# Expert stage of a mixture-of-experts block: four gather buffers instead of two, slots of four experts found ahead, late gathers in halves

## What is computed

```python
logits = x_flat @ Wr                                  # 12544 x 8
probs = softmax(logits, axis=0)                       # over the tokens
vals, idx = top_k(probs.T, 1024)                      # each of 8 experts picks 1024 tokens
selected = x_flat[idx]                                # gather
h = gelu(einsum('ecd,edf->ecf', selected, W1) + b1)   # 128 -> 512
out_e = einsum('ecf,efd->ecd', h, W2) + b2            # 512 -> 128
output = zeros.at[idx].add(vals[..., None] * out_e)   # scatter with add
```

## Time and profile before

| what | value |
|---|---|
| median of 3 runs | 534.93 us (534.64 to 538.28) |
| the profiled execution's own time | 540.0 us |
| its span, first to last instruction | 538.1 us |
| PE busy | 373.2 us (69%) |
| DVE busy | 320.3 us (60%) |
| ACT busy | 271.8 us (51%) |
| POOL busy | 167.6 us (31%), nearly all of it after 279 us |

### The profile page before, as it was taken

One profiled execution on the slowest core, in us unless ns is written; L12 is line 12 of the kernel. 1 busy time (PEld: TensorE's weight loads), 2 busy tenths in 40 slices (PEclk: granted clock), 3 DMA queues, 4 the chain that ended last, 5 costly groups with the idle time before them and its releaser, 6 DMA issues. The chain is left out here.

```text
span 538.1 us, 6516 instructions
## 1 busy us (share of the span) xinstructions
PE 373.2 (69%) x1532; PEld 227.4 (42%) x1532; DVE 320.3 (60%) x1059; ACT 271.8 (51%) x581; POOL 167.6 (31%) x153
## 2 busy tenths in 40 slices
PE   2989998999989976300026497897969595950565
PEld 2655665666666555200023253354434242410454
DVE  4578999999999885688864255444444220220354
ACT  3357888989889956766501246244435433400000
POOL 3000000000000000000017258787878788768000
PEclk9989999999999986555556699978879697995555
DMA  3413665454565333500002023434525243333898
GB/s 97 124 56 121 204 194 177 151 179 155 173 192 180 122 122 114 152 1 0 0 5 57 21 76 36 91 35 90 74 51 78 45 81 43 31 31 34 222 383 354
DMA packets 33957, 58.56 MB, mean 109 GB/s; under 512 B 5864, under 2 KB 18320, under 8 KB 33936
## 3 DMA queue, kind: packets, MB, share of 16 engines
q1 hardware_dynamic: 20016, 43.15, 25.4%
q0 software_dynamic: 11264, 8.66, 12.2%
q10 hardware_dynamic: 2656, 6.51, 3.2%
HBM read 28.02 MB, written 23.86 MB: 96 GB/s over the span
## 5 line engine op out<-in xcount | busy, mean ns | idle before, releaser
L374 POOL DMA_INDIRECT picked<-token_rows,gather_idx x64 | 62.0, 968 | 305.8 <-issue 292.1
L388 POOL DMA_INDIRECT moe_sum<-y_rows,scatter_idx x64 | 100.4, 1569 | 23.9 <-issue 23.3
L619 PE MATMUL psC<-x_pad,tap_diag 128*128 128x392 f32 x256 | 93.4, 509 | 8.9 <-ACT x_pad L515 8.8
L787 PE MATMUL psC<-hid,w 128*128 128x512 f32 x128 | 66.2, 676 | 0.4 <-issue 0.3
L900 DVE SCALAR_TENSOR_TENSOR conv<-x_pad,taps_w,conv 128x784 f32<-128x784 f32 x64 | 66.0, 1032 | 0.2
L619 PEld LDWEIGHTS psC<-x_pad,tap_diag 128*128 128x128 f32 x256 | 47.2, 194 | 40.6 <-ACT x_pad L515 7.9
L1181 DVE TENSOR_SCALAR y_T<-psC,b_T 128x256 f32<-128x256 f32 x32 | 14.0, 480 | 68.0 <-PE psC L787 68.0
L568 ACT ACTIVATE hid<-psB,b_T 128x512 f32<-128x512 f32 x32 | 22.0, 687 | 58.0 <-PE psB L778 38.1
L787 PEld LDWEIGHTS psC<-hid,w 128*128 128x128 f32 x128 | 27.6, 223 | 34.0 <-issue 34.0
L778 PE MATMUL psB<-picked_T,w 128*128 128x512 f32 x64 | 35.6, 668 | 9.2 <-ACT picked_T L548 8.9
L484 ACT ACTIVATE ln_tok<-psA,ln_sm 112x128 f32<-112x128 f32 x112 | 40.5, 459 | 2.7 <-DVE ln_sm L892 2.7
(11 more groups left out here) (195 smaller groups left out, 657.6 us busy)
## 6 DMA issues: line engine op xcount, KB each, us to landing
token_rows<-rows SPq DMA_DIRECT2D x16, 416.5 KB, 3.0
x_in<-in_x_dram SPq DMA_DIRECT2D x16, 392.0 KB, 3.7
x_res<-in_x_dram SPq DMA_DIRECT2D x16, 392.0 KB, 4.6
moe_sum<-zero_rows SPq DMA_DIRECT2D x16, 392.0 KB, 5.1
x_all<-x SPq DMA_DIRECT2D x16, 392.0 KB, 2.9
out_dram<-act ACTq DMA_DIRECT2D x16, 392.0 KB, 5.7
w<-in_L_ffn_W_dram SPq DMA_DIRECT2D x16, 256.0 KB
ln_tok<-moe_sum SPq DMA_DIRECT2D x8, 392.0 KB, 5.6
```

What stands on the lines that cost most here:

```text
L374: nc.gpsimd.indirect_dma_start(out=picked[:, q, b, :], out_offset=None, in_=rows_dram, in_offset=bass.IndirectOffsetOnAxis(ap=gather_idx[: ...
L388: nc.gpsimd.indirect_dma_start(out=y_dram, out_offset=bass.IndirectOffsetOnAxis(ap=scatter_idx[:, q, b:b + 1], axis=0), in_=y_rows[:, q, b ...
L619: ins = nc.tensor.matmul(psC[:, h, 0:HALF].rearrange("c (h w) -> c h w", w=W), tap_diag[:, n, :], x_pad_v[:, q, y0:y0 + LINES, dx:dx + W], ...
L787: ins = nc.tensor.matmul(psC[:, h, :], w2[:, q, f * C:(f + 1) * C], hid[:, f, h * HS:(h + 1) * HS], start=(f == 0), stop=(f == FT - 1))
```

## The change

- There are four gather buffers: the two of `picked`, and two made of `x_in` and `x_res`, which are free by then. Buffer is e % 4, and each has its own two semaphores.
- Indices have a place of their own for each expert (`slot_idx`), so the copy to `scatter_idx` and its waits go.
- Slots of experts 0 to 3 are found ahead on DVE. On PE, `ties(2)` and the first `turn_picked` come after all of expert 1's slots; the rest of the small matmuls of experts 2 and 3 stands in the two halves of expert 0's `hidden`. Experts 1 to 4 then find the slots of experts 4 to 7.
- POOL's order: gathers 0 to 3; scatter 0; gather 4; scatter 1; gather 5; scatter 2; first half of gather 6; scatter 3; second half of 6; scatter 4; first half of 7; scatter 5; second half of 7; scatter 6; scatter 7.
- Scatter 0 is a plain indirect write, without the add (`moe_sum` is zero then).
- In expert 6, `turn_picked` of expert 7 stands after `down` and `back`, and `down` and `back` go by halves; DVE's `weigh` follows that order.
- Python loops take the place of the chip's loops in the expert stage, on every engine.

```diff
+        slot_idx = sb("slot_idx", [128, E, SB], U32)
+        picked_in = [picked[:, 0, :, :], picked[:, 1, :, :]] + [
+            spare[:, :, :].rearrange("s q n -> s (q n)")[:, 0:SB * ROW].rearrange("s (b r) -> s b r", r=ROW)
+            for spare in (x_in, x_res)]
...
+            def gather(e, h):
+                k = e % AHEAD
+                if e >= AHEAD and h == 0:
+                    pool.wait_ge(s_pt, (e - AHEAD) * 2 + 2)
+                    pool.wait_ge(s_ge, e - AHEAD + 1)
+                pool.wait_ge(s_idx, e * 2 + h + 1)
...
+                    if e == 0:
+                        nc.gpsimd.indirect_dma_start(out=y_dram, out_offset=at, in_=y_rows[:, q, b, :],
+                                                     in_offset=None).then_inc(s_sca[q], 16)
+                    else:
+                        nc.gpsimd.indirect_dma_start(out=y_dram, out_offset=at, in_=y_rows[:, q, b, :],
+                                                     in_offset=None, compute_op=ALU.add).then_inc(s_sca[q], 16)
...
+            for e in range(AHEAD):
+                gather(e, 0)
+                gather(e, 1)
+            for e in range(3):
+                scatter(e)
+                gather(e + AHEAD, 0)
+                if e < 2:
+                    gather(e + AHEAD, 1)
+            scatter(3)
+            gather(6, 1)
+            scatter(4)
+            gather(7, 0)
+            scatter(5)
+            gather(7, 1)
+            scatter(6)
+            scatter(7)
...
-                if e:
-                    turn_picked(0, 0, 0, 0)
                 slot_ranks(e)
+            pe.wait_ge(s_idx, 4)
+            ties(2)
+            turn_picked(0, 0)
...
+                    slot_work, slots_of = {}, e + 3
+                    if e == 0:
+                        if h == 1:
+                            turn_picked(0, 1)
+                        slots_of = 2 + h
+                        slot_work = ({0: [slots_before], 3: [slot_ranks]},
+                                     {0: [first_ties], 1: [slots_before], 3: [slot_ranks]})[h]
+                    elif e + 3 < E:
+                        slot_work = ({2: [first_ties]}, {0: [slots_before], 3: [slot_ranks]})[h]
+                    hidden(e, q, h, slot_work, slots_of)
...
+                if e == E - 2:
+                    for h in range(2):
+                        turn_picked(e + 1, h)
...
-                nc.vector.tensor_copy(scatter_idx[:, q, :], gather_idx[:, q, :]).then_inc(s_si, 1)
```

More of the change, by code:

```diff
@@ L47 @@
 UNROLL = 5
+AHEAD = 4
 ENDS = 4
@@ L311, in _ @@
                 load_w(q, q)
[L312 to L315, removed]
+            for e in range(2, E):
+                sp.wait_ge(s_l2, (e - 1) * 2)
+                load_w(e, e % 2)
             sp.wait_ge(s_sca[0], 16 * SB * E // 2)
@@ L367, in _, with scatter @@
                            allow_small_or_imprecise_dtypes=True).then_inc(s_const, 1)
[L369 to L373, removed]
-                    nc.gpsimd.indirect_dma_start(
[L375 to L383, removed]
+            def gather(e, h):
[4 more added lines that the diff above has]
+                pool.wait_ge(s_idx, e * 2 + h + 1)
+                pool.sem_inc(s_pool, 1)
+                for b in range(4 * h, 4 * h + 4):
+                    nc.gpsimd.indirect_dma_start(
+                        out=picked_in[k][:, b, :], out_offset=None, in_=rows_dram,
+                        in_offset=bass.IndirectOffsetOnAxis(ap=slot_idx[:, e, b:b + 1], axis=0),
+                    ).then_inc(s_gat[h][k], 16)
+            def scatter(e):
+                q = e % 2
+                if e >= 1:
+                    pool.wait_ge(s_sca[1 - q], (e + 1) // 2 * (16 * SB))
                 for b in range(SB):
@@ L585, in _ @@
             act.wait_ge(s_sd, 9)
-            for q in range(2):
-                expert(q, q, 0, True)
-            with act.Fori(1, E // 2 - 1) as pair:
-                for q in range(2):
-                    expert(pair * 2 + q, q, pair, True)
-            for q in range(2):
-                expert(E - 2 + q, q, E // 2 - 1, q == 0)
+            for e in range(E):
+                expert(e, e + 1 < E)
             with act.Fori(0, B // ENDS) as turn:
@@ L780, in hidden @@
                     if f in after:
-                        after[f](e + 2)
+                        for work in after[f]:
+                            work(slots_of)
             def down(e, q, h):
@@ L823, in expert @@
                         down(e, q, h)
-                        back(e, h, another)
-            for q in range(2):
-                expert(q, q, 0, True, True)
-            with pe.Fori(1, E // 2 - 1) as pair:
-                for q in range(2):
-                    expert(pair * 2 + q, q, pair, True, True)
-            for q in range(2):
-                expert(E - 2 + q, q, E // 2 - 1, False, q == 0)
+                        back(e, h, False)
+                if e == E - 2:
+                    for h in range(2):
+                        turn_picked(e + 1, h)
+            for e in range(E):
+                expert(e, e % 2)
             pe.wait_ge(s_gelu, E * 2 * FT)
@@ L1165, in slots_d @@
                     dve.wait_ge(s_pd, e * 4 + 2 * h + 2)
[L1166 removed]
+                    nc.vector.scalar_tensor_tensor(slot_idx[:, e, blocks], s_p[:, blocks], float(TILES), ranks[:, blocks, P],
                                                    ALU.mult, ALU.add).then_inc(s_idx, 1)
[L1169 removed]
+            for e in range(AHEAD):
                 slots_a(e)
@@ L1207, in expert @@
                 bias_out(e, 0)
-                if last:
+                if e >= E - 2:
                     weigh(e, q, use, 0)
                 bias_out(e, 1)
-                if not last:
+                if e < E - 2:
                     weigh(e, q, use, 0)
                 weigh(e, q, use, 1)
-            for q in range(2):
-                expert(q, q, 0, True)
-            with dve.Fori(1, E // 2 - 1) as pair:
-                for q in range(2):
-                    expert(pair * 2 + q, q, pair, True)
-            for q in range(2):
-                expert(E - 2 + q, q, E // 2 - 1, False, q == 1)
+            for e in range(E):
+                expert(e, e % 2, e // 2)
             for q in range(2):
```

99 lines of the change are left out of this document (34 added, 65 removed).

## The result

| | before | after |
|---|---|---|
| median of 20 runs, us | 536.62 (534.19 to 538.54) | 532.90 (529.89 to 538.14) |
| ratio after / before, 95% interval | | 0.9929 (0.9911 to 0.9947) |
| profiled execution, us (span) | 540.0 (538.1) | 534.26 (532.5) |
| end of the last scatter, us | 498.10 | 491.87 |

The kernel is 3.7 us faster by its medians. Foretold were 11 us, 524.0 in a range of 519.5 to 532; 532.9 lies just outside it. The slowest run after, 538.14, is over 1.5% above the fastest and isn't in the ratio. The profiled pair shows 6.2 us less at the end of the last scatter, where 11.0 were forecast, so the account has to find 4.8 us.

What follows compares the result with a forecast made beforehand. POOL was taken as the bound from 313 us on. Saving 7.0 (gap) and 4.9 (plain scatter), with a new wait before scatter 7, ended 11.0 us earlier: 540.0 to 529.0 profiled, median 524, range 519.5 to 532.

Steps and rivals of the forecast that it cites:

- part 2: Scatter 0 on POOL: a plain scatter costs what a gather block does, 10.2 us instead of 15.1, saving 4.9 us.
- The rival that it costs as much as the adding one: Scatter 0: plain costs POOL as much as adding, so 4.9 us more, 528.8 us in all; chance 0.18.
- part 3: POOL's order with half gathers: saves 2.2 us between scatters 5 and 6, spent in a new wait ahead of scatter 7.
- part 4: Index copies on DVE, chip loops and SP's weight loads: dropping the copies and the loops' end save nothing, at no cost.
- part 1: POOL's 13.0 us gap ahead of expert 2's first gather: earlier indices shrink it to 6, saving 7.0 us.
- the two bounds: Gap ahead of expert 2's gather: 4.1 us, or 8.4 if DVE's 4.26 us wait for ties(2) comes again.
- Is scatter 0 then held by expert 0? I count nothing: Ahead of scatter 0: expert 0's y_rows ready at 325.0, up to 3 later; POOL wants it at 326.3; 0 us counted.
- the 4.9 and nearly all of the 3 for ties(3): Expert 0: hidden begins 4.9 us later, and up to 3 us more for PE's wait on ties(3) and its return.
- The forecast's list: POOL's blocks in the new order: scatter 0 from 326.3, gather 4 until 346.7, on to scatter 6 until 467.9.
- the pace rival: Other engines set the pace at 23.6 us an expert: expert 4 is 8.0 us late, 532 us in all; chance 0.14.
- the slower rival: Experts 1 to 4 at a pace of about 26 us: expert 4 is 17.6 us late, 541.5 us in all; chance 0.05.
- The forecast's own sign of being wrong: POOL's timeline: waits for y_rows ahead of scatters 1 to 4 would show the other engines setting the pace.

Runs made afterwards that it cites:

- e1: The changed kernel with scatter 0 adding again instead of plain: 526.98 us against 528.52 for the kernel before, ratio 0.9968.
- e5: The changed kernel run once more without edit, on the chip without late semaphores: 522.06 us against 529.54 for the kernel before, ratio 0.9864.
- e2: The kernel before with a plain scatter 0 and nothing else: 523.29 us, ratio 0.9901 to the kernel before.
- e13: The kernel before with only scatter 0 made plain, run again in another job: 524.21 us, ratio 0.9909 to the kernel before.
- e10: The changed kernel with gathers 6 and 7 whole, the last ahead of scatter 4: 538.41 us, ratio 0.9986 to the kernel before, on the second chip.
- e11: The changed kernel with expert 6 ordered as before, expert 7 turned ahead of its down projection: 548.01 us, ratio 1.0153 to the kernel before.
- e3: The kernel before with the expert stage's chip loops written out on each engine: 528.45 us, ratio 0.9998 to the kernel before.
- e7: The changed kernel with the down projection of experts 0 and 1 done twice: 530.87 us, ratio 1.0029 to the unchanged kernel before.
- e9: The kernel before run once more without edit, on the second chip: 539.12 us against 539.20, ratio 0.9990.
- e14: The changed kernel with scatter 1 ahead of gather 4 on POOL, a single run: 524.71 us against 529.81 for the kernel before.
- e15: The changed kernel without the gathers of experts 4 to 7, a single run: 501.51 us against 529.81 for the kernel before.

## Why the prediction was wrong

**Right from scatter 1 on: POOL is the bound.** From scatter 1 to scatter 7 it never idles, in both traces of the changed kernel. Ahead of that it idled 13.8 us net in the profile of after (4.5, 3.6 and 5.7), where the forecast had 6.

**Right: the plain scatter (part 2).** 0.97 us an instruction and 10.2 us a block, -4.9 as forecast, in e1 against e5, e2 and e13. The rival that it costs as much as the adding one fell. The Trainium skill (Collectives: The Full Stack, section Stop ④ — SDMA + CCE: where bytes move and the add happens) calls the add free; here it costs POOL 0.6 us for 128 rows (1.57 against 0.97), whatever it costs the DMA engines.

**Right in kind: part 3 and part 4.** The wait ahead of scatter 7 was 2.7 net where 4.1 was forecast (472 less the 467.9 at which scatter 6 ends), within the forecast's 2.2 to 5.6; it is made by y_rows as foretold. e10 and e11 show that halving and the new order of expert 6 each bring nothing without the other. The loops cost nothing (e3).

**Too careful: part 1.** The gap became 4.5 net, between the 4.1 and the 8.4 of the two bounds. But its reading was wrong: the 13.0 us were put down to the place of the small matmuls. With the same code they are 2.4 net when PE's semaphores are in time (e3), and the change's own gap is then 1.8 (e5). Of the 8.5 us that the profiled pair shows here, the new order itself has 0.6; the rest is lateness that no longer falls on this chain (8.3 us of it before; after, 2.5, from 299.08, when expert 2's ranks end on PE, to 301.60, when DVE takes them) and comes back ahead of scatters 0 and 1. That 4.5 fell between the two bounds is thus luck in part: undisturbed, it is below both.

**The step that failed: "Is scatter 0 then held by expert 0? I count nothing", and its neighbour, which wasn't asked.** The time of expert 0 was foretold well: 325 to 328, measured 327.7, with late semaphores in it as in the 320.07 of before from which it was counted (undisturbed, e5 against e13, the new order makes it 319.6 - 311.6 = 8.0 us later, the 4.9 and nearly all of the 3 for ties(3)). POOL wanted it at 324.35, not 326.3, since the gap was shorter; what the gap gave, the wait ahead of scatter 0 took. So these two together cost 8.1 net against the 6 forecast. The larger part is scatter 1, 5.7 us. The forecast's list has gather 4 end at 346.7, which is when POOL wants expert 1, and at its own pace of 20.6 us expert 1 is ready at 326 + 20.6 = 346.6. The margin there was nil. I looked for the margin at expert 4, where three later blocks had made it 4 us, and gave the pace rival 0.14 on that. At the pace of 23.6 that stood in the earlier trace rows expert 1 would already have been 3 us late; the pace was 26.3, the 26 of the slower rival, for that one expert, and 17 to 18 from then on. Both pace rivals assumed one pace for all experts. What happened is a third case: late for two experts, then quick. The forecast's own sign of being wrong, a wait for y_rows ahead of scatters 1 to 4, came at scatter 1.

**Where the 26.3 came from.** The cause next in line is shown: PE's semaphores come 5.0 and 7.6 us after the recorded end of the matmuls in experts 0 and 1. Without them the two waits are gone (e5); e7 shows that lateness of this size there is enough to make two such waits. The forecast had the row that tells of it, DVE's 4.26 us of "remote" in the earlier trace rows, and used it only to widen the gap. The waits view of the kernel before had more of the kind, 5.7 us at most:

```profile
ACT hid L568 <- remote: 11.3, 4, 5.7
DVE s_cmp L1161 <- remote: 10.1, 3, 4.6
ACT picked_T L548 <- remote: 9.4, 4, 5.7
```

A waits view with such rows says two things that the forecast missed: the undisturbed pace is shorter than 20.6 (it is 16.9, e5), and a hand-over with no margin will be hit by the next such wait.

The account closes by the undisturbed run. In e5 expert 1 is ready at 336.5 and POOL wants it at 341.3, 4.8 of margin. In the profile of after it is ready at 354.0, 17.5 later, while POOL was itself held up by 0.9 at its first gather, 2.7 in the gap and 3.6 ahead of scatter 0: 17.5 - 4.8 - 7.2 = 5.5, against the 5.7 measured.

**What stays open** is why the semaphores come late on one chip and not on the other, for the same program. That it is a matter of the expert stage's loops is excluded, as the changed kernel has none there and shows it. The granted clock doesn't tell them apart either: from 335 to 352 us it is 1.00 in e9, where DVE waits 6.00 us until 351.35, and 1.00 in e5, where nothing is late. Whether gathers, the loading of code or other transfers take part wasn't told: e14 and e15 were made for the gathers and ran where there was nothing to see, and no run was made for the loading of code.

**The median.** The profiled pair differs by 5.7 us and the medians by 3.7. The forecast carried the profiled execution's 5.1 us above the median over to the kernel after, whose own is only 1.4 above its median. With 20 runs of each, before's profile is 3.4 above.

## What to carry to other kernels

When an edit speeds up the engine that sets the pace, write down for every hand-over the time at which it will ask and the time at which the other side is ready, and look at the smallest margin of all, which here was the first one and not the one after four experts. A wait that no engine of the kernel ends is lateness that can fall on another instruction in the new order: take it out to see the true pace, and then ask what the new order loses if it falls where the margin is thinnest. And time the parts of a change one by one: here, with no late semaphores, the plain scatter alone gives 0.990 where the whole change gives 0.986.

## What the runs showed of the hardware

- PE's semaphores can reach DVE and ACT late: 2.5, 5.0, 7.6 and 8.3 us after the recorded end of the matmuls at the four places worked out above. Such waits end between 295 and 303, 314 and 328, 337 and 356, and 374 and 389 us of this program; later ones are 1.2 us at most, the last at 409.54 (0.77 us, e10). This was so on one chip (before 539.2 us), and in both profiled executions of the case, and not on another (before 528.5 to 529.8). The same kernel takes 2% longer on the one than on the other, and 10.4 of the 11.4 us by which its last scatter ends later are the wait that they lengthen ahead of expert 2's gather.
- An indirect DMA of 128 rows mostly takes POOL 0.95 to 0.97 us for a gather and for a plain scatter, and 1.55 to 1.57 for an adding one (the first of a block up to 1.63), with 0.30 between any two.
- An adding scatter that follows another starts 2.5 to 2.7 us after the last instruction of it in e10, and 2.5 to 4.1 in e15, which is the landing; the 5 us of a half gather between them hide it (scatters 5 and 6 in the profile of after).
